# A Mamba layer with a 4-bit feed-forward block: D term on TensorE, SiLU product on VectorE, block scale in another instruction

## What is computed

```python
xz = layernorm(x) @ in_proj_w.T ; x, z = split(xz)
x = silu(conv4(x) + conv_b)                       # causal, 4 taps, per channel
dt_r, B, C = x_proj(x) ; delta = softplus(dt_proj(dt_r) + dt_b)
s[t] = s[t-1] * exp(delta * A) + (delta * x) * B  # 16 states per channel
y = sum_n s * C ; y = y + x * Dskip ; y = y * silu(z)
x = x_in + y @ out_proj_w.T
# feed-forward, on layernorm(x); fp4() is blockwise:
scale = maximum(max(abs(block)) / 6.0, 1e-12)
block = round_to_grid(block / scale) * scale
h = silu(fp4(v) @ fp4(w_gate).T) * (fp4(v) @ fp4(w_up).T)
out = x + fp4(h) @ fp4(w_down).T
```

## Time and profile before

| | |
|---|---|
| median of 3 runs | 4576.72 us (4568.63 to 4577.6) |
| profiled execution, its own time | 4559.53 us |
| its span | 4557.4 us |
| mean granted clock of TensorE | 0.98 |
| busy: VectorE | 4430.2 us, 97% |
| busy: TensorE | 4062.7 us, 89% |
| busy: GpSimd | 3945.2 us, 87% |
| busy: ScalarE | 3647.9 us, 80% |

### The profile page before, as it was taken

How to read it: one execution, slowest core, us unless ns; L and a number is a source line. 1 busy time by engine, 2 the same in 40 slices (tenths; PEclk the granted TensorE clock), 3 DMA queues, 4 the chain that set the end, 5 groups by cost and what they waited for, 6 DMA issues and landing times. The chain is left out here.

```text
span 4557.4 us, 64901 instructions
## 1 busy us (share of the span) xinstructions
PE 4062.7 (89%) x18397; PEld 1949.4 (43%) x18732; DVE 4430.2 (97%) x5804; ACT 3647.9 (80%) x6807; POOL 3945.2 (87%) x2461
## 2 busy tenths in 40 slices
PE   5889899998999989899898888989899899898987
PEld 2234444444444444444444444444444444444444
DVE  7999999999999999999999999999999999999995
ACT  5888788887888878788787888878788788787874
POOL 6989898898988889888898888989889898888984
PEclk8999999999999999999999999999999999999999
DMA  4645455454544545444454454545445454554541
GB/s 122 206 166 175 164 164 172 161 169 164 168 160 166 170 165 168 166 162 164 163 175 163 153 169 164 168 159 177 157 162 177 158 168 164 166 167 158 175 160 34
DMA packets 288970, 739.07 MB, mean 162 GB/s; under 512 B 35686, under 2 KB 87014, under 8 KB 288614
## 3 DMA queue, kind: packets, MB, share of 16 engines
q1 hardware_dynamic: 286912, 732.75, 48.2%
q10 hardware_dynamic: 1702, 2.16, 0.2%
HBM read 709.61 MB, written 25.17 MB: 161 GB/s over the span
## 5 line engine op out<-in xcount | busy, mean ns | idle before, releaser
L747 POOL TENSOR_TENSOR prod<-state,cs 128x1024 f32<-128x1024 f32 x1024 | 2395.7, 2359 | 140.2 <-DVE state L991 138.5
L970 DVE TENSOR_TENSOR db<-db,du 128x512 f32<-128x512 f32 x1536 | 1036.9, 675 | 42.9 <-PE db L1035 28.5
L1050 PE MATMUL ybank<-prod,ident 64*64 64x512 f32 x4096 | 1047.1, 632 | 7.7 <-DVE state L991 6.1
L480 ACT ACTIVATE decay<-delta,aneg 128x512 f32<-128x512 f32 x1536 | 1049.2, 712 | 4.6 <-DVE state L991 2.4
L1050 PE MATMUL cross<-prod,ident 64*64 64x512 f32 x4096 | 1047.0, 632 | 0.0
L991 DVE TENSOR_TENSOR_SCAN state<-decay,carry,db 128x512 f32<-128x512 f32 x768 | 952.8, 1254 | 0.0
L991 DVE TENSOR_TENSOR_SCAN state<-decay,db 128x512 f32<-128x512 f32 x768 | 908.5, 1196 | 7.9 <-PE bank_b L1298 7.9
L1035 PE MATMUL db<-pieces,sel 128*128 128x512 bf16 x1242 | 486.2, 391 | 334.5 <-DVE state L991 332.7
L738 POOL TENSOR_TENSOR brow<-brow,du 128x512 f32<-128x512 f32 x512 | 646.3, 1273 | 0.0
L1035 PEld LDWEIGHTS db<-pieces,sel 128*128 128x128 bf16 x1536 | 147.8, 96 | 1164.5 <-DVE state L991 838.3
L480 ACT ACTIVATE db<-delta,aneg 128x512 f32<-128x512 f32 x512 | 350.7, 685 | 202.2 <-DVE state L991 202.2
(11 more groups left out here) (132 smaller groups left out, 7570.0 us busy)
## 6 DMA issues: line engine op xcount, KB each, us to landing
cs<-c_rows SPq DMA_DIRECT2D x1024, 512.0 KB, 4.3
brow<-b_rows SPq DMA_DIRECT2D x512, 256.0 KB, 3.3
xin<-in_hidden SPq DMA_DIRECT2D x128, 128.0 KB, 3.7
xres<-in_hidden SPq DMA_DIRECT2D x128, 128.0 KB, 4.5
out_x<-ot SPq DMA_DIRECT2D x128, 128.0 KB, 4.0
c_rows<-xdbl SPq DMA_DIRECT2D x128, 32.0 KB, 2.9
b_rows<-xdbl SPq DMA_DIRECT2D x128, 32.0 KB, 2.6
win<-in_win_t SPq DMA_DIRECT2D x1, 1024.0 KB, 5.0
```

The lines of the kernel that those rows point to most:

```text
L480: act.activation(out, delta[:, w.mod(2), :], ACT.Exp, scale=aneg[:, w.mod(HEADS), n:n + 1]).then_inc(done, 1)
L747: pool.tensor_tensor(prod[:, r, :, :], state[:, 2 * p:2 * p + 2, :], cs[:, c, :, :], ALU.mult).then_inc(weighted, 1)
L970: dve.tensor_tensor(t[:, :], t[:, :], du[:, gu % 2, :], ALU.mult).then_inc(db_done, 1)
L1050: last = pe.matmul((ybank, cross)[k][c * Q:(c + 1) * Q, :], ident[rows, rows], prod[rows, p % P_RING, k, :], start=(p == 0), stop=(k == 1 ...
```

## The change

Four things. (1) `block_scale` becomes a `scalar_tensor_tensor` whose second tensor is `least`, a column of 1e-12 in SBUF that is read with a step of zero, where it was a `tensor_scalar` with 1e-12 as a constant. (2) `uu * dsk` is no longer added by VectorE: 64x64 matmuls with diagonal blocks `ddiag` add it into `cross`. The first tap of the convolution is cut into its two 64x64 diagonal blocks, and the four small matmuls stand together; the other three taps stay whole. (3) VectorE multiplies `ybank` with `sz` in the instruction that took line 937's place; line 763 of GpSimd and its semaphore `yg_done` go, and `project` waits for `y_taken`. (4) All slots and the order within the steps are chosen anew, on all five engines.

```diff
+        least = sb("least", [1])
+        ddiag = sb("ddiag", [HEADS, Q])
...
@@ vector
             def block_scale(s):
-                return dve.tensor_scalar(s[:, 1, :], s[:, 0, :], 1.0 / 6.0, SCALE_MIN, ALU.mult, ALU.max)
+                return dve.scalar_tensor_tensor(s[:, 1, :], s[:, 0, :], 1.0 / 6.0,
+                                                least[0:s.shape[0], :].broadcast_to([s.shape[0], s.shape[2]]),
+                                                ALU.mult, ALU.max)
...
                 if w := due("scan", 22):
                     dve.wait_ge(joined, w.val(plus=1))
+                    dve.wait_ge(sz_done, w.val(plus=1))
                     wait(dve, op_mm, w.div(4, 4, -3))
-                    dve.scalar_tensor_tensor(yg[:, w.mod(8) // 4, w.mod(4), :], uu[:, w.mod(4), :], dsk[:, w.mod(HEADS):w.mod(HEADS) + 1],
-                                             ybank[:, :], ALU.mult, ALU.add).then_inc(y_taken, 1)
+                    dve.tensor_tensor(yg[:, w.mod(8) // 4, w.mod(4), :], ybank[:, :], sz[:, w.mod(4), :],
+                                      ALU.mult).then_inc(y_taken, 1)
...
-                if t := due("post", 16):
+                if t := due("post", 14):
                     dve.wait_ge(op_mm, t.val(plus=1))
...
+                        for r in range(2):
+                            rows = slice(r * Q, (r + 1) * Q)
+                            dve.tensor_scalar(ddiag[rows, h, :], ident[rows, rows], dsk[rows, h:h + 1], None,
+                                              ALU.mult).then_inc(a_ready, 1)
...
@@ gpsimd
-                if w := due("scan", 25):
-                    pool.wait_ge(y_taken, w.val(plus=1))
-                    pool.wait_ge(sz_done, w.val(plus=1))
-                    y = yg[:, w.mod(8) // 4, w.mod(4), :]
-                    pool.tensor_tensor(y, y, sz[:, w.mod(4), :], ALU.mult).then_inc(yg_done, 1)
...
+                if w := due("scan", 8):
+                    weigh(w, 2)
...
-                if w := due("scan", 4):
-                    weigh(w, 2)
...
@@ tensor
-            def conv_tap(v, taps):
+            def conv_tap(v, k):
...
-                for k in taps:
-                    last = pe.matmul(pbank[:, :], cdiag[:, v.mod(HEADS), k, :], x[:, k:k + CH],
-                                     start=(k == 0), stop=(k == TAPS - 1))
+                last = pe.matmul(pbank[:, :], cdiag[:, v.mod(HEADS), k, :], x[:, k:k + CH],
+                                 start=False, stop=(k == TAPS - 1), skip_group_check=True)
...
-                    pe.wait_ge(yg_done, t.div(4, 4, 4))
+                    pe.wait_ge(y_taken, t.div(4, 4, 4))
...
+                v, w = due("pre", 9), due("scan", 9)
+                if v:
+                    x = xearly if v.mod(PER) < HEADS else xlate
+                    pe.wait_ge(x_evac, v.val(2, 2))
+                if w:
+                    pe.wait_ge(u_done, w.val(plus=1))
+                for r in range(2):
+                    rows, others = slice(r * Q, (r + 1) * Q), slice((1 - r) * Q, (2 - r) * Q)
+                    if v:
+                        pe.matmul(pbank[rows, :], cdiag[rows, v.mod(HEADS), 0, rows], x[rows, 0:CH], start=True,
+                                  stop=False, tile_position=(r * Q, r * Q), skip_group_check=True)
+                    if w:
+                        pe.matmul(cross[others, :], ddiag[rows, w.mod(HEADS), :], uu[rows, w.mod(4), :],
+                                  start=False, stop=False, tile_position=(r * Q, (1 - r) * Q), skip_group_check=True)
```

More of the change, by code:

```diff
@@ new lines, in step @@
+                if w := due("scan", 8):
+                    decay_of(w, 9)
+                if w := due("scan", 8):
+                    decay_of(w, 12)
+                if w := due("scan", 8):
+                    decay_of(w, 14)
+                if w := due("scan", 5):
+                    decay_of(w, 10)
+                if t := due("post", 21):
+                    act.wait_ge(v_norm, t.val(plus=1))
+                    wait(act, h_op, t.val(2))
+                    act.activation(bank_b[:, 0:DM], v2, ACT.Abs, scale=POWER).then_inc(v_abs, 1)
@@ new lines, in step @@
+                if v := due("pre", 13):
+                    act.preload_act_table_set("silu_and_others")
+                    h = v.mod(HEADS)
+                    act.wait_ge(conv_mm, v.val(plus=1))
+                    wait(act, y_taken, v.val(plus=-3))
+                    wait(act, du_done, v.val(plus=-3))
+                    wait(act, xd_mm, v.val(plus=-3))
+                    act.activation(uu[:, v.mod(4), :], pbank[:, :], ACT.Silu, bias=cb[:, h:h + 1]).then_inc(u_done, 1)
+                    act.wait_ge(z_mm, v.val(plus=1))
+                    act.activation(sz[:, v.mod(4), :], bank_a[:, :], ACT.Silu).then_inc(sz_done, 1)
+                    act.preload_act_table_set("exp_and_others")
@@ L621, in step @@
+                if w := due("scan", 2):
+                    decay_of(w, 6)
+                if w := due("scan", 2):
                     decay_of(w, 7)
[L622 removed]
+                if w := due("scan", 2):
                     decay_of(w, 8)
[L624 to L631 removed]
@@ L1182, in side @@
-                if t := due("post", 38):
-                    up(t, 1)
-                if t := due("post", 27):
-                    pe.wait_ge(v_quant, t.val(plus=1))
-                    if peeled and t.val() == 0:
-                        pe.wait_ge(xnt_done, 11)
-                    else:
-                        wait(pe, h_op, t.val(2))
-                    for k in range(KM):
-                        last = pe.transpose(bank_b[:, k * P:(k + 1) * P], v2_eps[:, k * P:(k + 1) * P], ident[:, :])
-                    last.then_inc(v_tp, 1)
@@ new lines, in side @@
+                if t := due("post", 26):
+                    pe.wait_ge(v_quant, t.val(plus=1))
+                    if peeled and t.val() == 0:
+                        pe.wait_ge(xnt_done, 11)
+                    else:
+                        wait(pe, h_op, t.val(2))
+                    for k in range(KM):
+                        last = pe.transpose(bank_b[:, k * P:(k + 1) * P], v2_eps[:, k * P:(k + 1) * P], ident[:, :])
+                    last.then_inc(v_tp, 1)
+                if v := due("pre", 10):
+                    conv_tap(v, 1)
```

568 lines of the change are left out of this document (270 added, 298 removed).

## The result

| | before | after |
|---|---|---|
| median, us | 4577.16 (4568.63 to 4580.9, 4 runs) | 4272.48 (4269.07 to 4281.67, 4 runs) |
| ratio, 95% interval | | 0.934 (0.932 to 0.936) |
| profiled execution and its span | 4559.53, 4557.4 | 4271.48, 4269.6 |
| mean granted clock of TensorE | 0.98 | 0.992 |

What follows compares the result with a forecast made beforehand. VectorE, busy 97%, was taken as the bound. From 4559.5 us, the scales take 130 off, the finished sum 8, and TensorE's cover adds 13: 4434.5, or 4452 as a median; range 4265 to 4570.

Steps and rivals of the forecast that it cites:

- What bounds the kernel: VectorE, busy 97%, sets the span; line 838's scales hold 2.32 us per unit of waiting for GpSimd, 297 us in all.
- The form of the scale: In `block_scale`, the new scalar_tensor_tensor waits for GpSimd like the old form: worth 0, with 297 us as the other end.
- The first rival: The new form of the scale escapes the wait for GpSimd: 4297 us, chance 25%.
- Where the vs scale falls: With pair 2 behind `v_norm`, the scale of v waits 0 to 0.1 us: 1.1 us less per unit.
- the second rival: GpSimd's inverse root stays late and the vs scale meets pair 1, making the kernel slower: 4659 us, chance 12%.
- the forecast's sign: GpSimd idle before line 803 for over 2 us a unit, with vs at 0.15 to 0.3 us, would confirm the vs step.
- Where the hs scale falls: The scale of h starts 0.7 to 1.2 us into GpSimd's pair 5 and waits 1.25 us on average, before 1.15.
- TensorE's cover: In early units VectorE's products wait more for B from TensorE: 0.2 us for each of 64 units, 13 us in all.
- The finished sum: Line 937 on VectorE becomes a product taking 675 ns instead of 734: 8 us less.
- the D term: Four quarter matmuls on TensorE replace one whole tap: 0.09 us more per unit, 12 us in all, hidden.
- The fourth rival: The four quarter matmuls run one after another and TensorE bounds the early units: about 4540 us, chance 7%.
- GpSimd's 163 us at nothing: GpSimd's dropped line 763, 163.2 us beside VectorE's work, is worth nothing but the shift counted for the hs scale.

Runs made afterwards that it cites:

- b_stt: The kernel before with nothing but the scale as scalar_tensor_tensor and its column `least`: 4562.85 us, ratio 0.998.
- a_ts: The changed kernel with block_scale as tensor_scalar again, everything else as changed: 4284.73 us, ratio 0.937 against the kernel before.
- a_copyb: The changed kernel with the copy of the B row for state 1 issued at slot -6 rather than -3: 4393.46 us, ratio 0.961 against the kernel before.
- b_none: The kernel before without the two block_scale instructions of the loop, so rounded values differ: 4203.82 us, ratio 0.920.
- b_act: The kernel before with both scales formed by ScalarE as x/6 + 1e-12 instead of by VectorE: 4490.77 us, ratio 0.984.
- b_pair2: The kernel before with only GpSimd's pair 2 (weigh) issued behind `v_norm` and the drive of state 9, slot 6 instead of 4: 4486.85 us, ratio 0.979.
- a_old23: The changed kernel with the old D term, the old finished sum and line 763 on GpSimd: 4433.64 us, ratio 0.970 against the kernel before.
- b_best: The kernel before with the hs scale on ScalarE at slot 45 and pair 2 moved behind `v_norm`: 4226.35 us, ratio 0.924.

## Why the prediction was right and where it failed

- **What bounds the kernel** was right: VectorE at 97 to 98% before and after, and the oddity of line 838 was the thing to read.
- **The form of the scale** was right: taken as 0, it is 8 us (b_stt) to 12 us (a_ts), of 297 at the other end. The first rival, with 25% and a price 25 us off the result, fell only by these two runs. The Trainium skill ("SBUF — State Buffer", "Who interferes with whom") has an instruction of VectorE with two SBUF inputs contend with one of GpSimd that reads SBUF. Here that held also for a second input of one column read with a step of zero: 1348 and 1392 ns in b_stt.
- **Where the vs scale falls** was right in its price: 143 us forecast (1.17 - 0.05 in 128 units), 145.2 measured. The root was not late; the second rival did not come. But the forecast's sign, GpSimd idle before line 803 for over 2 us a unit, did not show: it was 1.1, and pair 1 ended within about 0.2 us of the scale's start in most units. Had GpSimd been a few tenths later, each scale would have waited for that much of the pair; that it wasn't is luck. In a_copyb, where no copy holds GpSimd back and the hs scale holds VectorE, the idle time is 3.0 us (383.9 in 128 units), as the forecast had in mind; that fits the step that failed, which comes next.
- **Where the hs scale falls** is the step that failed. It took the wait as 1.25 us; it was 0.26 (447 ns less 189). (1.25 - 0.26) x 128 = 127 us, the most of what was missed. The sum of GpSimd's instructions from `v_norm` to pair 5 left out the copy of the B row: its issue moved from slot -8 to -3, and the drive ahead of pair 5 now waits for it. I had 15.0 us between the two; it was 16.5 in this unit (2038.17 to 2054.70), and 1.37 of that is the wait; on the mean it was 16.3, and 15.2 in a_copyb. VectorE's side, 15.7 to 16.2, was right: 16.0 to 16.1. I wrote that a shift by 0.8 us would make the scale slip in before the pair, and kept its 0 as a bound; the shift was there to be read. a_copyb removes it and finds the 1.25 (1435 less 190).
- **TensorE's cover** had the wrong sign: 13 us more of idle time forecast, 28.5 less measured. The idle time before the products with B fell from 42.9 to 13.7 us (line 969 against the earlier trace rows), which is as much. I had let shorter units press on TensorE. The runs show no press, and no new slot is needed for the gain: in the old slots it is 3.6 us in b_none and 4.6 in b_act, and still 26.2 in b_pair2, which frees the vs scale alone. So in the old slots it went with the waits of the scales, that of hs above all; in the new ones a_copyb brings the hs wait back and has 8.8. By what way a scale's wait makes a later product late stays open. This and the last point together are 127 + 41 = 168 us, against a miss of 4434.5 - 4271.5 = 163; the other lines of VectorE, 6.9 us dearer, take most of the difference back.
- **The finished sum** (8 forecast, 7.0 measured) and **the D term** were right. Line 1225 is busy for 66.6 + 65.6 us and line 1228 for 131.2, 1.03 us each in a unit, and the two lie on one another, as the four quarters of the earlier trace rows do. In the late unit above:

```profile
2043.48 0.60 PE L1225 MATMUL pbank<-xlate,cdiag 64*64 64x512 f32 x2
2043.50 0.60 PE L1228 MATMUL cross<-uu,ddiag 64*64 64x512 f32 x2
```

  The fourth rival did not come. The rule of the Trainium skill ("TensorEngine Tiling (Array Packing)", "Restrictions and Gotchas"), by which two row tiles cannot access one bank together, is not borne out here either: both blocks of the tap write `pbank`, start within 0.01 us of one another, and the next four matmuls follow 0.43 us later.
- **GpSimd's 163 us at nothing** stood for the changed kernel's sum, but a_old23 shows that the new order rests on parts 2 and 3. Of the cover I had only said "beside VectorE's work", not how near GpSimd is to its limit in the new order.
- **The range** held by luck. The forecast's own part of it, 4310 to 4560, doesn't follow from its bounds: an hs wait of 0 takes 1.25 x 128 = 160 us off and gives 4292, one of 2.3 adds 134 and gives 4586. The result, 4272, lies below either; only the first rival, which did not come, reached that far down.

What stays open: which slot of the new table costs the 65 us by which b_none beats a_none. The runs show only that VectorE's loss there stands in front of `gated`, behind TensorE.

## What to carry over

A tiny instruction whose mean is eight times its least is standing in a lock, and the profile counts that as busy: look at least, median and most, and at what runs on the other engine at its end. Take such a wait apart by phase, with every instruction and every copy that moves between two points of both engines; a transfer issued three slots earlier cost 121 us here. Where the phase is that fragile, move the instruction to an engine that doesn't share the way, or its neighbour behind its consumer, rather than hope for the gap.

## What the runs showed of the hardware

- Removing 146 us of GpSimd's waiting for a copy made the kernel 121 us slower; GpSimd then waited 240 us more for VectorE (a_copyb).
- VectorE's wait ends 0.13 to 0.14 us before the end of GpSimd's instruction, with a pair of 2.35 us and with a drive of 1.27 us. The most was 4859 ns (b_pair2), through the tail of a drive and two pairs: GpSimd can go on with its next instruction before VectorE gets its turn.
- ScalarE's activation on 44 columns took 314 to 332 ns in all 128 units of b_best, with GpSimd busy for 93% of the span: it does not wait as VectorE's does.
